# Row maxima of two heads by one VectorE operation, and the last layer's additions to x on VectorE, in a four-layer transformer kernel

## What is computed

```
h = _rmsnorm(x, g1) * (1.0 + scale1[:, None, :]) + shift1[:, None, :]
x = x + _mha(h, w_qkv, b_qkv, w_ao, b_ao, n_head)
h = _rmsnorm(x, g2) * (1.0 + scale2[:, None, :]) + shift2[:, None, :]
x = x + _ffn(h, w_fc, b_fc, w_fo, b_fo)
```

## Time and profile before

| | us |
|---|---|
| median of three runs (lowest, highest) | 2264.01 (2261.25, 2267.37) |
| the profiled execution, its own time | 2262.32 |
| span of the profiled execution | 2260.4 |
| PE busy | 2155.1 (95%) |
| DVE busy | 1697.4 (75%) |
| ACT busy | 1249.8 (55%) |
| POOL busy | 1086.4 (48%) |

### The profile page before, as it was taken

How to read it: one execution, slowest core, us unless ns; L and a number is a source line. 1 busy time by engine, 2 the same in 40 slices (tenths; PEclk the granted TensorE clock), 3 DMA queues, 4 the chain that set the end, 5 groups by cost and what they waited for, 6 DMA issues and landing times.

```text
span 2260.4 us, 63283 instructions
## 1 busy us (share of the span) xinstructions
PE 2155.1 (95%) x20080; PEld 1807.2 (80%) x20080; DVE 1697.4 (75%) x4339; ACT 1249.8 (55%) x2618; POOL 1086.4 (48%) x1333
## 2 busy tenths in 40 slices
PE   4699999999999999999999999999999999999997
PEld 2488888888888888888878888888778888787877
DVE  2677777777776777677778777777788888888873
ACT  1366666666565555555676666666654454435441
POOL 2244455455544454445454554446454545444434
PEclk7799999999999999999999999999999999999998
DMA  5422112222222112212331122222222121111210
GB/s 194 131 72 73 63 63 68 70 71 77 85 91 71 62 60 70 74 61 81 102 99 64 60 69 75 66 63 74 86 72 73 55 67 58 63 60 61 65 58 15
DMA packets 164671, 166.11 MB, mean 73 GB/s; under 512 B 29296, under 2 KB 143856, under 8 KB 164560
## 3 DMA queue, kind: packets, MB, share of 16 engines
q1 hardware_dynamic: 164560, 164.69, 22.7%
HBM read 58.47 MB, written 4.39 MB: 28 GB/s over the span
## 4 chain that ended last, share of the span: by engine, by line
PE 84%; DVE 6%; issue 3%; SPq 2%; ACT 1%; POOL 1%; DMA 1%; POOLq 0%; ACTq 0%; DVEq 0%
PE B L530 36%; PE B L630 14%; PE B L799 10%; PE B L776 7%; PE B L577 7%; PE B L639 4%; PE B L649 2%; PE B L733 2%; DVE NEGM L1018 2%; SPq L1407 2%; PE B L554 2%; DVE G L1025 1%; ACT PR L944 1%; ACT G L912 0%; POOL GHl L1300 0%
## 5 line engine op out<-in xcount | busy, mean ns | idle before, releaser
L944 ACT ACTIVATE PR<-B 128x512 f32<-128x512 f32 (+1 forms) x1024 | 504.9, 570 | 282.8 <-PE B L776 280.1
L1300 POOL TENSOR_TENSOR GHl<-G,GHh 128x256 fp32r<-128x256 f32 x512 | 377.6, 738 | 475.2 <-ACT GHh L918 288.4
L1018 DVE TENSOR_REDUCE NEGM<-B 128x2 f32<-128x512 f32 x768 | 485.0, 683 | 91.9 <-PE B L577 91.9
L530 PE MATMUL B<-H2h,W1h 128*128 128x256 f32 x1280 | 397.8, 311 | 3.1 <-issue 3.1
L530 PE MATMUL B<-H2h,W1l 128*128 128x256 f32 x1280 | 363.2, 284 | 0.0
L530 PE MATMUL B<-H2l,W1h 128*128 128x256 f32 x1280 | 362.7, 283 | 0.0
L918 ACT ACTIVATE G<-B,VEC 128x256 f32<-128x256 f32 x384 | 182.0, 474 | 284.2 <-PE B L530 284.2
L630 PE MATMUL B<-W2h,GHh 128*128 128x256 f32 x1024 | 297.1, 290 | 1.7 <-POOL GHl L1300 1.7
L630 PE MATMUL B<-W2l,GHh 128*128 128x256 f32 x1024 | 290.3, 283 | 0.0
L630 PE MATMUL B<-W2h,GHl 128*128 128x256 f32 x1024 | 289.6, 283 | 0.0
L530 PEld LDWEIGHTS B<-H2h,W1h 128*128 128x128 f32 x1280 | 244.3, 191 | 44.4 <-issue 26.4
(11 more groups left out here) (160 smaller groups left out, 4704.1 us busy)
## 6 DMA issues: line engine op xcount, KB each, us to landing
QS<-QHL SPq DMA_DIRECT2D x768, 64.0 KB, 2.1
KS<-KHL SPq DMA_DIRECT2D x768, 64.0 KB, 2.1
GA<-gate_scratch SPq DMA_DIRECT2D x48, 256.0 KB, 3.2
GM<-gate_scratch SPq DMA_DIRECT2D x48, 256.0 KB, 3.4
RAW<-in_w SPq DMA_DIRECT2D x36, 256.0 KB, 3.5
CW<-in_cw SPq DMA_DIRECT2D x3, 1536.0 KB, 12.4
QS<-MT SPq DMA_DIRECT2D x256, 4.0 KB
GA<-in_rows_last SPq DMA_DIRECT2D x16, 256.0 KB, 3.3
```

The costliest lines, as they stand in the source:

```text
L530: last = nc.tensor.matmul(dst, w[i], x[j], start=(first_k and n == 0), stop=(last_k and n == 2))
L944: nc.scalar.activation(PR[:, h % PRING].rearrange("p k q -> p (k q)")[:, 0:n], src[:, 0:n], ACT.Exp, scale=SCALE).then_inc(ac_exp, 1)
L1018: last = nc.vector.tensor_reduce(NEGM[:, :, c], src, op=ALU.max, axis=AX.X, negate=True)
L1300: nc.gpsimd.tensor_tensor(GH[1][:, j % RING, :], G[:, j % RING, :], GH[0][:, j % RING, :].bitcast(F32), ALU.subtract).then_inc(po_gl, 1)
```

## The change

Three things are edited.

1. In layers 0, 2 and 3 (no causal mask) the maxima of the two heads of a pair are taken by one `tensor_reduce` over two neighbouring banks (4, 5 or 0, 1), for pairs 0 to 6; pair 7 lies in banks 0 and 2 and keeps two operations. `outputs_lo` now stands behind both maxima of pair 0. The semaphore rises by 2 at the end of a pair.
2. In layer 3 VectorE adds the PSUM bank to x itself (`add_to_x`), for the output projection and for the MLP. GpSimd's adds of TOK are gone there, and its bias adds move to j = 1 and j = 3. `statistics_2` moves to j = 5 behind pair 3, `rstd` of norm 2 to the front of what follows GpSimd's blocks, `normalise_2` ahead of the rotation of the query.
3. The store waits for dv_dn and not po_x2.

```diff
+                def maxima_of_pair(p):
+                    banks = S_BANKS[2 * p:2 * p + 2]
+                    src = B[:, banks[0]:banks[1] + 1, :].rearrange("p h (i k) -> p h i k", i=NT)
+                    c = HB * (p // HQ) + p % HQ
+                    dst = NEGM[:, :, c:c + HQ + 1:HQ].rearrange("p i h -> p h i")
+                    dv.wait_ge(pe_s, H * s.a + 2 * p + 2)
+                    if p == 0:
+                        at_least(dv, pe_mt, 2 * s.na)
+                    nc.vector.tensor_reduce(dst, src, op=ALU.max, axis=AX.X, negate=True).then_inc(dv_max, 2)
...
                 def maxima(p):
-                    if s.a is not None:
+                    if s.a is not None and (s.la == CAUSAL or p == HP - 1):
                         maximum(2 * p)
                         maximum(2 * p + 1)
+                    elif s.a is not None:
+                        maxima_of_pair(p)
...
                     if j == 3:
-                        if s.a is not None:
+                        if s.a is not None and s.la == CAUSAL:
                             maximum(0)
+                        elif s.a is not None:
+                            maxima_of_pair(0)
                         if s.r is not None:
                             outputs_lo()
-                        if s.a is not None:
+                        if s.a is not None and s.la == CAUSAL:
                             maximum(1)
                         maxima(1)
...
-                            multiply(s, bank(WO_BANK), GA, sp_ga, s.r, s.lr).then_inc(dv_wo, 1)
+                            if s.lr == ROPE:
+                                add_to_x(s.sr, po_xb1, s.r, bank(WO_BANK)).then_inc(dv_wo, 1)
+                            else:
+                                multiply(bank(WO_BANK), GA, sp_ga, s.r).then_inc(dv_wo, 1)
                         maxima(2)
                     if j == 5:
                         maxima(3)
+                        if s.lr == ROPE:
+                            statistics_2()
...
                     dv.wait_ge(pe_dn, NJ * s.m + NJ)
-                    at_least(dv, po_x1, s.r_done)
-                    multiply(s, bank(7), GM, sp_gm, s.m, s.lm).then_inc(dv_dn, 1)
+                    if s.lm == ROPE:
+                        add_to_x(s.sm, po_xb2, s.m, bank(7)).then_inc(dv_dn, 1)
+                    else:
+                        if s.lr != ROPE:
+                            at_least(dv, po_x1, s.r_done)
+                        multiply(bank(7), GM, sp_gm, s.m).then_inc(dv_dn, 1)
                 maxima(7)
...
-                statistics_2()
+                if s.lr != ROPE:
+                    statistics_2()
                 if s.lq == ROPE:
                     r = s.q - NSEQ * ROPE
+                    if s.lr == ROPE:
+                        normalise_2()
                     rotate(s, pe_q, 1, G, V_BQ, V_BQR, 0)
...
-                    normalise_2()
+                    if s.lr != ROPE:
+                        normalise_2()
...
+            def add_to_x(sequence, s_bias, n, src):
+                x = X[:, seq(sequence), :, :].rearrange("p a t d -> p (a t) d")
+                dv.wait_ge(s_bias, n + 1)
+                apart(dv)
+                return nc.vector.tensor_tensor(x, x, src, ALU.add)
...
-                    if j == 4 and s.r is not None:
+                    if j == (1 if s.lr == ROPE else 4) and s.r is not None:
                         residual_1_bias(s)
-                    if j == 5 and s.r is not None:
+                    if j == 3 and s.lm == ROPE:
+                        residual_2_bias(s)
+                    if j == 5 and s.r is not None and s.lr != ROPE:
                         residual_1(s)
                     if j == NJ - 2:
                         low_1(s)
-                if s.m is not None:
+                if s.r is not None and s.lr == ROPE:
+                    rstd(MV2, RS2, TV2, dv_mv2, po_t2, po_rs2, s.r, s.lr)
+                if s.m is not None and s.lm != ROPE:
...
             def store(s, tile, sequence):
-                hold(po_x2, tile + 1)
+                hold(dv_dn, tile + 1)
```

More of the change, by code:

```diff
@@ L1009, in maximum @@
                         at_least(dv, pe_mt, 2 * s.na)
[L1010 to L1019 removed]
+                    if s.la != CAUSAL:
+                        nc.vector.tensor_reduce(NEGM[:, :, c], src, op=ALU.max, axis=AX.X, negate=True).then_inc(dv_max, 1)
+                        return
+                    apart(dv)
+                    for i in range(NT):
+                        keys = (i + 1) * P
+                        unmasked = MASK[:, 0].rearrange("p b c -> p (b c)")[:, T - keys:T]
+                        last = nc.vector.tensor_tensor_reduce(src[:, i, 0:keys], src[:, i, 0:keys], unmasked, -1.0,
+                                                              HIGHEST, ALU.add, ALU.min, NEGM[:, i, c:c + 1])
+                    last.then_inc(dv_max, 1)
+                def maxima_of_pair(p):
[7 more added lines that the diff above has]
+                    nc.vector.tensor_reduce(dst, src, op=ALU.max, axis=AX.X, negate=True).then_inc(dv_max, 2)
                 def hidden(j):
@@ L1079, in normalise_1, with statistics_2 @@
                     normalise(XQ, tokens(sequence), MV1, RS1, dv_xn1, layer == ROPE)
+                def statistics_2():
+                    if s.r is not None:
+                        if s.lr == ROPE:
+                            dv.wait_ge(dv_wo, s.r + 1)
+                            apart(dv)
+                        else:
+                            dv.wait_ge(po_x1, s.r + 1)
+                        statistics(tokens(s.sr), ST2, MV2, dv_st2, dv_mv2, s.r)
                 for j in range(NJ):
@@ L1195, in body, with multiply @@
                     evacuate(1)
-            def multiply(s, src, rows, s_rows, n, layer):
-                if layer == ROPE:
-                    return nc.vector.tensor_copy(TOK[:], src)
+            def add_to_x(sequence, s_bias, n, src):
+                x = X[:, seq(sequence), :, :].rearrange("p a t d -> p (a t) d")
+                dv.wait_ge(s_bias, n + 1)
+                apart(dv)
+                return nc.vector.tensor_tensor(x, x, src, ALU.add)
+            def multiply(src, rows, s_rows, n):
                 dv.wait_ge(s_rows, 16 * (n + 1))
@@ L1286, in residual_1_bias, with residual_2_bias @@
                 nc.gpsimd.tensor_tensor(x, x, GA[:, 1:2, :].to_broadcast([P, NT, D]), ALU.add).then_inc(po_xb1, 1)
+            def residual_2_bias(s):
+                x = x_of(s.sm)
+                po.wait_ge(dv_xn2, s.m + 1)
+                po.wait_ge(sp_gm, 16 * (s.m + 1))
+                apart(po)
+                nc.gpsimd.tensor_tensor(x, x, GM[:, 1:2, :].to_broadcast([P, NT, D]), ALU.add).then_inc(po_xb2, 1)
             def residual_1(s):
@@ L1320, in body @@
                 split_lo(po, nc.gpsimd.tensor_tensor, po_w, split_in(s, LATE))
-                if s.r is not None:
+                if s.r is not None and s.lr != ROPE:
                     rstd(MV2, RS2, TV2, dv_mv2, po_t2, po_rs2, s.r, s.lr)
```

23 lines of the change are left out of this document (5 added, 18 removed).

## The result

The changed kernel is **slower**, by 0.8%: 2281.3 us median of five runs (2278.2 to 2284.2) against 2261.3 of five runs of the kernel before on the same chip (2259.1 to 2267.4). The timed ratio, with its 95% interval in brackets, is 1.0077 [1.0059, 1.0095], or +17.4 us of 2261; the two medians taken by themselves lie 20.0 us apart. The profiled execution has a span of 2279.4 us where the one before had 2260.4: +19.0. The sign was forecast, and so was about half of the size: +9.6 of +17.4.

The account below looks back on a forecast made before the run. TensorE alone was taken to bound layers 0 and 2, with some 1.2 us idle a step in layer 3. Terms 12.9 + 3.5 - 3.0 + 0.5 - 3.0 - 1.3 = +9.6 us on 2264.0, given as 2273.5; range 2260 to 2281.

Parts of the forecast that it names:

- The pair, 1.21 us, and the place behind it: VectorE's fused maximum takes 1.21 us, the next operation starts 1.13 after it; outputs_lo behind pair 0 moves 0.53 us.
- Layers 0 and 2, +12.9: TensorE's output projection waits for the later outputs_lo: 0.46 us a step in layer 0, 0.53 in layer 2.
- The bound I gave, 15.6: Upper limit of the loss in layers 0 and 2: 2 x 13 x 0.60 us.
- Late scores in layer 3, +0.56: Scores 14 and 15 wait for pair 5's end, 0.53 us later; with 0.03 for pair 7, transposes move 0.56 a step.
- Given back in layer 3, -0.29: outputs(2) comes closer behind the transposes, 2.08 us for 2.37; a step nets +0.27, 13 steps +3.5.
- The nop and wait ahead of `add_to_x` are hidden in the other steps: In steps not priced singly, the nop and wait before VectorE's addition to x cost nothing.
- The floor of 2.08 us: In layer 3 outputs(2) stands at best 2.08 us behind the norm 2 transposes, 2.37 before the change.
- Step 49, -3.0: GpSimd's variance of norm 2 goes first: 1.4 us of wait and 1.6 us of slow clock go.
- Behind step 62, -3.8: Late scores in step 63 +0.5, earlier norm 2 in step 64 -3.0, last add of TOK off the store's path -1.3.
- The start and steps 15 to 34, 0: No term in the sum; loss covered by weight splits in steps 15, 32, 33, 34; layer 1 keeps its own maxima.
- The rule against the trace: Skill's no-start-until-empty rule would save 1.1 us a step by pairing, the trace's overlap 0.5; neither reaches TensorE-bound layers.
- more is lost: Rival, chance 0.10: second pair's lateness reaches the transposed scores, nothing of the features' wait returns: +17.7, 2282 us.

Follow-up runs that it names:

- pairs alone: The kernel before with only the fused maxima of the change, the last layer's residuals left as before; timed ratio 1.0110.
- pair 5 single: The changed kernel with pair 5's two maxima as single operations, pairs 0 to 4 and 6 still fused; timed ratio 1.0072, then 1.0055.
- the second pair of profiles: The kernel before and the changed kernel, both unedited, each profiled once more; spans 2261.2 and 2277.5 us.

## Why the prediction was half right

- **The pair, 1.21 us, and the place behind it: right.** 1.218 measured, and pairs back to back start 2.35 - 1.22 = 1.13 us apart, as forecast. Layers 0 and 2 lost by the place of `outputs_lo`: with it ahead of the fused pair 0, 14.3 of 15.85 us came back, and with the old order and a single pair 0 the steady steps were as before.
- **Layers 0 and 2, +12.9: it was +15.85.** Each step lost 0.58 and 0.64 us for 0.46 and 0.53. The sum took the start of pair 0 for that of maximum 0. But the pair started 0.10 us later behind the scores, as its second wait did not fold into the operation, and putting that wait first gave the 0.10 back. The bound I gave, 15.6, was passed by 0.25; the pair's late start is larger than that.
- **Late scores in layer 3, +0.56: right.** 0.52 with the pairs alone, 0.53 back with pair 5 single.
- **Given back in layer 3, -0.29: it was -0.11.** The step that failed is "The nop and wait ahead of `add_to_x` are hidden in the other steps". The floor of 2.08 us was met to the hundredth. But the addition stands directly between the late matmuls and the last maxima, and its second wait, nop and address computation run after the wait that ends last: 0.18 us, half of which came back when the wait and the nop were moved ahead; that the rest is the address computation is likely, but no run shows it by itself. A steady step is 0.44 us longer for the forecast 0.27. That the 13 steps came to +4.3, near +3.5, is in part luck: the eleven steps between the first and the last make +4.8, and step 50, the first, is 0.48 shorter (39.47 for 39.95), which the sum did not have.
- **Step 49, -3.0: it was 0.0,** and +1.3 in the second pair of profiles (38.1 for 36.8). I followed the variance, which did move ahead, and not the other input of norm 2. In step 49 the second residual is still layer 2's, so norm 2 waits for GpSimd's addition to x; the change also puts norm 2 ahead of the rotation, so everything on VectorE waits with it, and it then collides with the weight split that the variance had passed. This was the largest single miss, and the text had all the pieces: the diff keeps the wait for `po_x2` where `s.lm != ROPE`. With norm 2 in its old place in that one step, three profiles give -0.2 to -1.8.
- **Behind step 62, -3.8: right,** -3.74.
- **The start and steps 15 to 34, 0: +2.9 and -0.6** in these two profiles. They don't repeat. The unchanged kernel moves by 2.4 us over steps 0 and 1 and by 1.2 in step 34. The timed +17.4 is near to what the steps explain: 15.85 + 4.3 - 3.74 = 16.4.

- **The rule against the trace** was read by half. The measured starts are 1.13 us apart, as the trace before gave them, so no term hung on it; the last section says what the skill's section adds.

Of the rivals, "more is lost" came nearest in size (2282) and not in mechanism: the features' wait did come back. The range's upper end, 2281, stood 0.3 us under the median: three terms were too small by 3.0, 3.0 and 0.8 us, all in the same direction.

## What to carry to other kernels

When two operations become one, the later half's price is paid by whoever waited for the earlier half and by whatever stood between them; look there first, since an engine with time to spare gains nothing by being faster. When an operation moves ahead of others on its queue, list every semaphore that it waits for in every kind of step, the transitions between layers too, not the one that the move was made for. Ahead of an operation on the critical chain, order the waits so that the one that ends last stands last, with as little as possible to compute behind it. A single step whose TensorE clock can differ from one execution to the next is not to be judged from one profile.

## What the runs showed of the hardware

- A wait that has long been met cost 0.09 to 0.10 us a step on VectorE where it stood behind the wait that ended last (32.10 and 32.29 us a step), and nothing that shows ahead of it (32.01 and 32.20; 0.64 us from scores to pair, 0.63 to the single maximum before). The addition to x, with a second wait, a nop and an address computation ahead of it, starts 0.17 us later behind the scores than the copy did (1.64 for 1.47), and 0.10 with the wait and the nop moved ahead (1.57).
- Two VectorE instructions that took 0.61 us took 2.58, and two others 2.62 for 0.87, each beside two GpSimd subtractions of weights of 1.3 us each, which took 2.59 and 2.72 us for the 2.53 of the kernel before. In the changed kernel's step 49 the GpSimd pair ends at 1672.36 and the VectorE pair at 1672.51. The Trainium skill, page "SBUF — State Buffer", section "Who interferes with whom", says that the two engines share a port pair as an exclusive lock and that the one that comes second waits for the whole instruction; here VectorE came second both times and ended 0.15 us (1672.51 - 1672.36) and 0.28 us (1657.07 - 1656.79) behind, so the trace agrees.
- Fused maxima overlap with what follows as single ones do: 2.35 us for two pairs of 1.22, which would take 2.44 one behind the other. The Trainium skill, page "VectorE: DVE Perf Modes", section "The DRAIN you can't avoid", says that the next operation does not start until the pipe is empty, and adds that one that is not held starts earlier. The trace shows the second case, for pairs and for single maxima, so it does not contradict the section, as the prediction had it.
- TensorE's clock in a stretch with a stall is not fixed by the kernel. In step 34 of the kernel before, it stood still for 2.08 us (1158.37 to 1160.45) and stayed at a granted clock of 1.00 (2.4 GHz). In the second profile of the same kernel it stood still from 1158.29 to 1160.14 in the same place, for 1.85 us, and ran at a granted clock of 0.50 (1.2 GHz) from 1160.99 to 1164.40; the means are 0.86 in the 4 us stretch and 0.72 in the next. The windows of the first, then of the second:

```profile
1158.26:1162.26 4.00, 1.92 (x17) 1.84 (x16) 4.00 (x8) 1.45 (x5) 2.10 (x2) 1.00 0.41 148
1162.26:1166.26 4.00, 4.00 (x39) 3.49 (x37) 3.26 (x7) 2.97 (x6) 3.00 (x4) 1.00 0.02 6
```

```profile
1158.14:1162.14 4.00, 2.14 (x15) 2.03 (x14) 4.00 (x8) 1.56 (x4) 1.99 (x2) 0.86 0.47 159
1162.14:1166.14 4.00, 4.00 (x29) 3.47 (x28) 2.89 (x6) 1.66 (x5) 1.95 (x2) 0.72 0.01 4
1160.99:1164.40 3.41, 3.41 (x22) 2.88 (x20) 2.30 (x5) 1.68 (x4) 2.06 (x3) 0.50 0.02 6
```
